# The opening of the first attention: one value group moved to the fifth pair, four masks with buffers of their own, and copies issued ahead of exponentials

## The reference, cut to what matters

```python
x = x + xattn0(layernorm(x), ctx, ctx, mask, Wq, Wk, Wv, Wo)   # 4 batches x 512 rows, 256 wide, 16 heads of 64
x = x + ffn0(layernorm(x), ...)                                # 8 experts, top-k by expert
x = x + xattn1(layernorm(x), ctx, ctx, ...)                    # banded, 16 heads of 16
x = x + ffn1(x, ...)                                           # 8 experts in 4 groups
# xattn0:
Qh, Kh, Vh = (q @ Wq, k @ Wk, v @ Wv)            # split into 16 heads
energy = einsum('nqhd,nkhd->nhqk', Qh, Kh) / 8
energy = where(mask == 0, -1e20, energy)
out = einsum('nhqk,nkhd->nqhd', softmax(energy), Vh).reshape(n, t, 1024) @ Wo
```

## Time and profile before

| | us |
|---|---|
| median of 3 runs | 1238.46 (1237.23 to 1240.76) |
| the profiled execution, its own time | 1239.35 |
| its span in the trace | 1237.6 |
| first attention | from 0 to about 510 |
| PE busy over the span | 1090.5 (88%) |
| mean granted clock of PE, of full speed | 0.938 |

### The profile page before, as it was taken

One profiled execution on the slowest core, in us unless ns is written; L12 is line 12 of the kernel. 1 busy time (PEld: TensorE's weight loads), 2 busy tenths in 40 slices (PEclk: granted clock), 3 DMA queues, 4 the chain that ended last, 5 costly groups with the idle time before them and its releaser, 6 DMA issues. The chain is left out here.

```text
span 1237.6 us, 28697 instructions
## 1 busy us (share of the span) xinstructions
PE 1090.5 (88%) x10304; PEld 807.7 (65%) x10305; DVE 743.5 (60%) x2145; ACT 684.8 (55%) x1300; POOL 516.9 (42%) x574
## 2 busy tenths in 40 slices
PE   5799999999999999975799996889898553999996
PEld 2567777777777777765488873445454242888885
DVE  5677876787778878756411045677776521555553
ACT  4788876787778777745422233576666211433331
POOL 4676455445554333210347620866665122121112
PEclk9899999999999999965899998999999765999998
DMA  9322222222212222164446556144442232111110
GB/s 312 88 69 54 53 70 69 53 53 70 66 48 60 55 53 53 27 206 139 125 147 192 152 136 207 52 122 121 137 127 75 95 95 69 27 30 26 21 27 10
DMA packets 89675, 111.01 MB, mean 90 GB/s; under 512 B 9744, under 2 KB 69904, under 8 KB 89424
## 3 DMA queue, kind: packets, MB, share of 16 engines
q1 hardware_dynamic: 82544, 100.88, 27.9%
q0 software_dynamic: 7008, 8.49, 3.9%
HBM read 59.93 MB, written 24.77 MB: 68 GB/s over the span
## 5 line engine op out<-in xcount | busy, mean ns | idle before, releaser
L638 DVE TENSOR_TENSOR e_t_lo<-et,e_t_hi 128x512 f16<-128x512 f32 x256 | 176.6, 690 | 55.4 <-ACT e_t_hi L558 52.9
L664 DVE CUSTOM_DVE_ANT_0 masked<-sc,mask_bias 128x512 f32<-128x512 f32 x256 | 175.6, 686 | 52.9 <-issue 39.1
L565 ACT ACTIVATE e<-masked,neg_max 128x512 f32<-128x512 f32 x256 | 184.3, 720 | 38.8 <-DVE neg_max L664 38.0
L558 ACT ACTIVATE e_t_hi<-et 128x512 f16<-128x512 f32 x256 | 151.9, 593 | 83.6 <-PE et L460 82.3
L460 PEld LDWEIGHTS et<-ident,e 128*128 128x128 f32 x1024 | 126.2, 141 | 53.6 <-ACT e L565 5.4
L460 PE MATMUL et<-ident,e 128*128 128x128 f32 x1024 | 154.5, 274 | 0.7 <-DVE e_t_lo L638 0.4
L1749 ACT ACTIVATE d_e<-d_st 128x384 f32<-128x384 f32 (+1 forms) x192 | 93.8, 526 | 50.4 <-PE d_st L1836 45.7
L84 PE MATMUL ob<-v_lo,e_t_hi 128*128 128x65 f16 x1024 | 119.5, 193 | 0.0
L83 PE MATMUL ob<-v_hi,e_t_hi 128*128 128x65 f16 x1024 | 119.3, 193 | 0.0
L85 PE MATMUL ob<-v_hi,e_t_lo 128*128 128x65 f16 x1024 | 118.7, 193 | 0.0
L2195 POOL DMA_INDIRECT out<-h_res,h_token x22 | 34.1, 1550 | 167.4 <-DVE h_res L2247 162.0
(11 more groups left out here) (393 smaller groups left out, 2800.5 us busy)
## 6 DMA issues: line engine op xcount, KB each, us to landing
kk<-nat_k SPq DMA_DIRECT2D x64, 256.0 KB, 3.5
raw<-in_fc SPq DMA_DIRECT2D x16, 1024.0 KB, 7.6
qq<-nat_q SPq DMA_DIRECT2D x64, 128.0 KB, 2.5
mask_raw<-in_mask SPq DMA_DIRECT2D x16, 256.0 KB, 3.5
scratch_stack<-kq_hi SPq DMA_DIRECT2D x16, 256.0 KB, 3.1
scratch_stack<-kq_lo SPq DMA_DIRECT2D x16, 256.0 KB, 3.2
q<-scratch_stack SPq DMA_DIRECT2D x32, 128.0 KB
k<-scratch_stack SPq DMA_DIRECT2D x32, 128.0 KB
```

The costliest lines, as they stand in the source:

```text
L558: nc.scalar.activation(e_t[u % NBUF].hi[:], et[u % 2][:], ACT.Copy).then_inc(turned_hi, 1)
L565: nc.scalar.activation(e[u % NBUF][:], masked[u % NBUF][:], ACT.Exp, bias=neg_max[:, g % 2, j:j + 1], scale=-1.0).then_inc(exp_ok, 1)
L638: nc.vector.tensor_tensor(e_t[u % NBUF].lo[:], et[u % 2][:], e_t[u % NBUF].hi[:], ALU.subtract).then_inc(turned_lo, 1)
L664: nc.vector.tensor_tensor_reduce(masked[u % NBUF][:], sc[j % 2][:], mask_bias[g // PAIRS % 2][:, j % QT, :], -SCALE0, 3e38, ALU.add, ALU.m ...
```

## The change

- **V groups.** V(1,0) moves from unit 4 of the first pair to unit 6 of the fifth pair. V(0,4) and V(0,6) move from units 0 and 1 to units 2 and 3.
- **Masks.** Masks 0 to 3 get four raw buffers (the two old ones and the two output tiles `o`) and semaphores of their own; masks 2 and 3 are loaded without waiting for POOL, right after `stack(0)`. Masks from 4 on use the two old buffers as before. POOL's place for mask 4 (unit 2) and SP's (behind `stack(1)`) are unchanged.
- **Parts.** `wv_b` is loaded after the masks instead of before `stack(0)`, and `ctx1` after `wk_b` and `wq_b`. High and low parts are made at units 3, 5, 6, 9, 13, 17, 21, 25, 29 and 33 (`SPLIT_AT0`). V(1,1), at unit 12, becomes the first group that needs `ctx1`. The constants of the second V tile move to the third pair.
- **ACT's order.** The high part of `wv_b` no longer stands before the first V group; in the first pair's units the copies out of `pj` stand ahead of the exponential.
- **DVE's order.** The low parts of Q0 and V(0,0) move ahead of one set of layer norm statistics each; that of V(0,2) moves behind the first maximum.

```diff
--- before.py
+++ after.py
@@ -93,14 +93,14 @@
         return "k", g + 1
     if j == 1 and g + 1 < PAIRS0:
         return "q", g + 1
-    if j == 4 and b + 1 < B:
+    if j == 4 and b + 1 < B and (b, p) != (0, 0):
         return "v", (b + 1, p)
     if j == 5 and b >= 1 and 1 <= p <= QT:
         return "w", (b - 1, p - 1)
     if j == 5 and b + 1 < B and p in NORM_PAIRS:
         return "z", (b + 1, p - NORM_PAIRS[0])
-    if j == 6 and b == 0 and p < QT:
-        return "v", (0, 2 * p + 1)
+    if j == 6 and b == 0 and p <= QT:
+        return "v", (0, 2 * p + 1) if p < QT else (1, 0)
     if j == 7 and g >= 1:
         return "t", g - 1
     return None
@@ -108,7 +108,7 @@
 
 def opening_work(u):
 
-    return ("v", (0, 2 * u + 4)) if u < 2 else None
+    return ("v", (0, 2 * u)) if 2 <= u <= 3 else None
 
 
 def is_direct(what):
@@ -131,11 +131,10 @@
 
 GROUP0, COPY0, ADD0, DIRECT0, ORDER0 = number_groups()
 EARLY = ("ctx0", "wk_a", "wq_a")
-PARTS0 = EARLY + ("wv_a", "wv_b", "ctx1", "wk_b", "wq_b", "wk_c", "wq_c", "ctx2", "ctx3", "wo_a", "wo_b")
+PARTS0 = EARLY + ("wv_a", "wv_b", "wk_b", "wq_b", "ctx1", "wk_c", "wq_c", "ctx2", "ctx3", "wo_a", "wo_b")
 PART0 = {name: n for n, name in enumerate(PARTS0)}
-SPLIT_LOW = {1: "wv_b", 2: "ctx1", 3: "wk_b", 5: "wq_b", 9: "wk_c", 12: "wq_c", 17: "ctx2", 20: "ctx3", 25: "wo_a", 28: "wo_b"}
-SPLIT_HIGH = {u: name for u, name in SPLIT_LOW.items() if name != "wv_b"}
-NEEDS = {("k", 2): "wk_b", ("q", 2): "wq_b", ("k", 4): "wk_c", ("q", 4): "wq_c", ("v", (1, 0)): "ctx1", ("v", (2, 0)): "ctx2", ("v", (3, 0)): "ctx3",
+SPLIT_AT0 = {3: "wv_b", 5: "wk_b", 6: "wq_b", 9: "ctx1", 13: "wk_c", 17: "wq_c", 21: "ctx2", 25: "ctx3", 29: "wo_a", 33: "wo_b"}
+NEEDS = {("k", 2): "wk_b", ("q", 2): "wq_b", ("k", 4): "wk_c", ("q", 4): "wq_c", ("v", (1, 1)): "ctx1", ("v", (2, 0)): "ctx2", ("v", (3, 0)): "ctx3",
          ("k", PAIRS): "ctx1", ("k", 2 * PAIRS): "ctx2", ("k", 3 * PAIRS): "ctx3", ("w", (0, 0)): "wo_b", ("v", (0, 1)): "wv_b"}
 
 
@@ -170,7 +169,8 @@
         scores, masked_ok, exp_ok = sem("scores"), sem("masked_ok"), sem("exp_ok")
         turned, turned_hi, turned_lo, pv_done = sem("turned"), sem("turned_hi"), sem("turned_lo"), sem("pv_done")
         rden_ok, normed = sem("rden_ok"), sem("normed")
-        mask_in, bias_ok = [sem(f"mask_in{i}") for i in range(2)], sem("bias_ok")
+        mask_in, bias_ok = [sem(f"mask_in{i}") for i in range(QT + 2)], sem("bias_ok")
+        early_masks = [mask_raw[0][:], mask_raw[1][:]] + [part[:].rearrange("p t d -> p (t d)").bitcast(I32) for part in o]
         last_turned, last_hi, last_lo, late_full = (sem(n) for n in ("last_turned", "last_hi", "last_lo", "late_full"))
         before_last = GROUP0["t", PAIRS0 - 2] % 2
         late = [sc[0], sc[1], pj[before_last], ob[0][:].rearrange("p t d -> p (t d)")]
@@ -243,9 +243,10 @@
             @block.sync
             def _(sp):
                 def load_mask(n):
-                    if n >= 2:
-                        sp.wait_ge(bias_ok, n - 1)
-                    sp.dma_start(mask_raw[n % 2][:], dram["mask"][n // QT, (n % QT) * P:(n % QT + 1) * P, :]).then_inc(mask_in[n % 2], 16)
+                    if n >= QT:
+                        sp.wait_ge(bias_ok, n - 3 if n < QT + 2 else n - 1)
+                    dst, done = (early_masks[n], mask_in[n]) if n < QT else (mask_raw[n % 2][:], mask_in[QT + n % 2])
+                    sp.dma_start(dst, dram["mask"][n // QT, (n % QT) * P:(n % QT + 1) * P, :]).then_inc(done, 16)
 
                 def stack(g):
                     i = g % 2
@@ -282,14 +283,10 @@
                 load_x(2)
                 load_mask(1)
                 load_x(3)
-                load_part("wv_b")
                 stack(0)
                 load_mask(2)
-                load_part("ctx1")
-                load_part("wk_b")
-                load_part("wq_b")
                 load_mask(3)
-                for name in ("wk_c", "wq_c", "ctx2", "ctx3", "wo_a", "wo_b"):
+                for name in ("wv_b", "wk_b", "wq_b", "ctx1", "wk_c", "wq_c", "ctx2", "ctx3", "wo_a", "wo_b"):
                     load_part(name)
                 for g in range(PAIRS0 - 1):
                     stack(g + 1)
@@ -299,10 +296,13 @@
             @block.gpsimd
             def _(pool):
                 def bias(n):
-                    pool.wait_ge(mask_in[n % 2], 16 * (n // 2 + 1))
+                    if n < QT:
+                        pool.wait_ge(mask_in[n], 16)
+                    else:
+                        pool.wait_ge(mask_in[QT + n % 2], 16 * ((n - QT) // 2 + 1))
                     if n >= 2 * QT:
                         pool.wait_ge(masked_ok, (n // QT - 1) * PAIRS * UNITS)
-                    pool.tensor_scalar(mask_bias[n // QT % 2][:, n % QT, :], mask_raw[n % 2][:], 0.0, MASKED, ALU.is_equal, ALU.mult).then_inc(bias_ok, 1)
+                    pool.tensor_scalar(mask_bias[n // QT % 2][:, n % QT, :], early_masks[n] if n < QT else mask_raw[n % 2][:], 0.0, MASKED, ALU.is_equal, ALU.mult).then_inc(bias_ok, 1)
 
                 def split(what):
                     kind, at = what
@@ -321,8 +321,8 @@
                         b, ct = at // PAIRS, at % PAIRS
                         if b >= 2:
                             pool.wait_ge(pj_full, GROUP0["w", (b - 2, QT - 1)] + 1)
-                        if b < 2:
-                            pool.wait_ge(part_lo, PART0["wq_b" if at == 0 else "wq_c" if at == 1 else "wo_b"] + 1 - len(EARLY))
+                        if b < 2 and at >= 1:
+                            pool.wait_ge(part_lo, PART0["wq_c" if b == 0 else "wo_b"] + 1 - len(EARLY))
                         hi, lo = o_t[b % 2].hi[:, ct, :], o_t[b % 2].lo[:, ct, :]
                     else:
                         pool.wait_ge(stacked[0], STACKED * at)
@@ -354,9 +354,9 @@
                         what = side_work(g, j)
                         if what in COPY0:
                             split(what)
-                        if g * UNITS + j in SPLIT_LOW:
-                            low_part(SPLIT_LOW[g * UNITS + j])
-                        if (g, j) == (0, 3):
+                        if g * UNITS + j in SPLIT_AT0:
+                            low_part(SPLIT_AT0[g * UNITS + j])
+                        if (g, j) == (2, 3):
                             pool.wait_ge(part_lo, PART0["ctx1"] + 1 - len(EARLY))
                             fill_constants(1)
                         if j == 2 and g // PAIRS + 1 < B and g % PAIRS < QT:
@@ -595,15 +595,14 @@
                 high_part("wv_a")
                 direct_high(("k", 0))
                 direct_high(("q", 0))
-                high_part("wv_b")
                 direct_high(("v", (0, 0)))
+                direct_high(("v", (0, 2)))
                 root(slice(QT, NT), 1)
-                direct_high(("v", (0, 2)))
                 units = PAIRS0 * UNITS
                 for u in range(units + TURN_LAG):
                     if u >= TURN_LAG:
                         turned_part(u - TURN_LAG)
-                    if u < units:
+                    if UNITS <= u < units:
                         exponent(u)
                     what = side_work((u - 1) // UNITS, (u - 1) % UNITS) if 1 <= u <= units else None
                     if what in COPY0:
@@ -612,8 +611,10 @@
                         direct_high(what)
                     if 1 <= u <= units and opening_work(u - 1) is not None:
                         direct_high(opening_work(u - 1))
-                    if u in SPLIT_HIGH:
-                        high_part(SPLIT_HIGH[u])
+                    if u < UNITS:
+                        exponent(u)
+                    if u in SPLIT_AT0:
+                        high_part(SPLIT_AT0[u])
                     ahead = side_work(u // UNITS, u % UNITS + 2) if u < units and u % UNITS == 3 else None
                     if ahead is not None and ahead[0] == "z":
                         b, i = ahead[1]
@@ -707,17 +708,17 @@
                     nc.vector.tensor_tensor(T.z_t.lo[:, :, cols], et[i][:].rearrange("p (c t) n -> p c (t n)", c=DT), T.z_t.hi[:, :, cols], ALU.subtract).then_inc(z_lo, 1)
                 statistics(1)
                 direct_low(("k", 0))
+                direct_low(("q", 0))
                 statistics(2)
-                direct_low(("q", 0))
+                direct_low(("v", (0, 0)))
                 statistics(3)
                 variances(later_tiles, 1)
-                direct_low(("v", (0, 0)))
-                direct_low(("v", (0, 2)))
                 units = PAIRS0 * UNITS
                 for u in range(units + TURN_LAG):
                     if u < units:
                         maximum(u)
                     if u == 0:
+                        direct_low(("v", (0, 2)))
                         scales(later_tiles, 1)
                     if u >= TURN_LAG:
                         turned_part(u - TURN_LAG)
```

## The result

| | before | after |
|---|---|---|
| median of 5 runs, us | 1238.46 (1237.23 to 1240.76) | 1246.11 (1244.38 to 1248.70) |
| the profiled execution's own time | 1239.35 | 1245.61 |
| span of that execution | 1237.6 | 1243.9 |
| ratio of the times | | 1.0064, 95% interval 1.0044 to 1.0084 |

The prediction, 1239.2 in a range of 1235.4 to 1243.0, was wrong: the sign was right, and so was the wait that it named, but the loss was 7.65 us and not 0.7.

What follows compares the result with a forecast made beforehand. It took PE as the bound, deciding when PE leaves its last long opening hole and with how much work ahead: 3.2 us later, minus 2.46 us, is +0.7, so 1238.46 + 0.7 = 1239.2 us, range 1235.4 to 1243.0.

Steps and rivals of the forecast that it cites:

- the sign: Whole kernel: slightly slower, 1238.46 + 0.7 = 1239.2 us.
- the wait that it named: First pair: POOL waits for mask 4's DMA, so PE idles before V(0,1) until 41.2 us, against 38.02 for V(1,0) before.
- The mechanism: Opening: mask 4 delays wv_b's low part and V(0,1) by 3.2 us; 2.46 us less work remains; half clock costs the same.
- the forecast of +0.7: Opening: PE resumes 3.2 us later with 2.46 us less work ahead, difference +0.7 us; chance 0.70.
- Mask 4's landing: DMA queue, first pair: mask 4 lands at 37.0 us, between 36.2 and 38.2, giving -0.1 to +1.9 us overall.
- V(1,1) and `ctx1`: Unit 12: POOL's step ends at 58.55, PE arrives at 59.17; 0.6 us of cover, up to 0.6 us if gone.
- The parts at units 13, 21 and 29: Parts made a few units later (13 to 33): same instructions, 2.13 us each on POOL, idle half the time; counted at nothing.
- The queue drains slowly: Slower rival: at 261 GB/s mask 4 lands at 41.7 us, PE starts at 45.9; +5.4 us, 1243.9; chance 0.12.
- The change does nothing to POOL's start: Rival: Q1 copy stays late, mask 4 issued at 35, landing at 37.8 us; +1.5 us, 1240; chance 0.08.
- Mask 4 doesn't queue: Faster rival: mask 4 lands at 31.8 us, PE starts at 36.1; -4.4 us, 1234.1; chance 0.10 together with no wait, 1231.
- The chance given to a loss: Whole kernel slower by over 0.3%: 0.12, and 0.02 for the forecast's upper tail; within 0.3%: 0.76.
- V(1,1) first: Condition for being wrong: PE waits again after 45 us, at V(1,1) before any other place.

Runs made afterwards that it cites:

- lows_first: Changed kernel with POOL taking mask 4 at unit 7 instead of unit 2 in the first pair; median 1241.22 us, ratio to the kernel before 1.0019.
- parts_late: Changed kernel with ctx2, ctx3, wo_a and wo_b loaded behind stack(1) and mask 4 instead of ahead; median 1242.87 us, ratio to before 1.0028.
- filled: Changed kernel with 48 products of 512 columns, result overwritten, added before the wait of V(0,1); median 1244.53 us, ratio to before 1.0048.
- v10_alone: Kernel before with only V(1,0) moved to unit 6 of the fifth pair; median 1234.10 us, ratio to before 0.9961.
- parts_at12: Changed kernel with mask 4 and ctx1 at unit 7, four parts behind mask 4, and wk_c, ctx2, wo_a at units 12, 20, 28; 1229.59 us, ratio 0.9930.
- all_three: Changed kernel with mask 4 and ctx1 at unit 7, and ctx2, ctx3, wo_a, wo_b loaded behind mask 4; median 1229.16 us, ratio to before 0.9911.
- ctx1_at7: Changed kernel with high and low part of ctx1 made at unit 7 instead of unit 9; median 1243.33 us, ratio to before 1.0038.

## Why the prediction was wrong

**The mechanism was right.** Mask 4's transfer became the last thing on POOL's way to `wv_b` (lows_first, parts_late), V(0,1) took the place of V(1,0) as the group that waits, half clock followed for as long as before in the profiled execution (filled has its price), and V(1,0) cost its 1.3 us later (v10_alone).

**Two terms were wrong, and a small one was missed.** Against the forecast of +0.7:

- *Mask 4's landing, +2.9.* The sum had 37.0, POOL began at 39.97 (38.58 to 40.40 in the four other executions with these loads, so +1.6 to +3.4). This is the step that failed first: "the DMA engines, not SP, set when this is through, at about 34.3" assumed that the new order moves the same bytes by the same time. By 34 us it had moved 0.6 MB less (295 against 313 GB/s), which is 1.7 us at 350 GB/s. I had capped the loss at 1.2 us, and then taken next to nothing of it. Why the bytes were fewer is shown only as far as the time: all of it was lost before 19 us, most of it from 14 to 16 us (86 against 359 GB/s), where the queue ran dry ahead of the first `kk`. The rest, about 1.2 us, is between the last bytes and the landing: 0.4 us as before was assumed, but the stages of the changed kernel show a tail:

```profile
37.00:38.00 1.00, 0.00 (x0) 0.00 (x0) 0.00 (x0) 0.00 (x0) 0.00 (x0) 0.50 0.99 269
38.00:39.00 1.00, 0.00 (x0) 0.00 (x0) 0.00 (x0) 0.00 (x0) 0.00 (x0) 0.50 0.26 86
39.00:40.00 1.00, 0.00 (x0) 0.00 (x0) 0.00 (x0) 0.00 (x0) 0.03 (x1) 0.50 0.03 10
```

  A transfer has landed when all 16 of its landing signals are in. The trace has those of mask 4 from 38.27 to 39.22, and the last alone at 39.89; before, all 16 came between 37.33 and 37.77. So the mean share is low there, 0.26 and 0.03, while the last engines still work.
- *V(1,1) and `ctx1`, +3.1.* This is a misread row. I took the V group at 59.17 for V(1,1) and found 0.6 us of cover. The group at 59.17 is V(0,3), of unit 14; V(1,1), of unit 12, is at 55.42 (two units of 1.23 and one group of 1.30 earlier, which is 3.75 us):

```profile
55.42 0.38 PE L83 MATMUL pj<-wv_hi,ctx_t_hi 128*128 128x512 f16 x1
```

  Against the end of POOL's step, 58.55, the cover is 55.42 - 58.55 = -3.1 us. The profile of before held this number to about a tenth (measured wait: 3.06). The mistake was not to count units from a known one to the row in hand.
- *The parts at units 13, 21 and 29, +0.7.* "The same instructions, hidden" was false for ACT: three waits of 0.45 grew to 0.70 to 0.72. parts_at12 shows the cause: one unit earlier, ACT's high part no longer follows the copy of a V group, and the waits are back at 0.45.

0.7 + 2.9 + 3.1 + 0.7 = 7.4, against a mark of 7.5 and 7.65 by the medians. That the sum agrees so well with both is in part luck: the ratio's interval is 2.5 us either way, and the first term alone differs by 1.8 us between executions.

Three smaller readings were off without effect, because mask 4's landing covered them: POOL ended masks 2 and 3 at 25.5 and not at 24, both splits at 29.1 and not at 27.8, and mask 4 was issued at 31.93 and not at 29.0.

**The rivals.** "The queue drains slowly" was the slower rival; its direction was right for mask 4 (39.9, not 41.7), but mask 4 alone would have left the time at about +3.6. "The change does nothing to POOL's start" fell: the splits ended 4.6 us earlier. "Mask 4 doesn't queue" fell with the 8.0 us from its issue to its landing and with parts_late. The sentence of the Trainium skill behind it (DMA: Bandwidth & Descriptors, Queues, rings and completion order) says two things: each engine takes its descriptors in ring order, and completion is not in order per issuing engine. With the first parts_late agrees, as far as one landing time can tell. Of the second no run here has a case in which mask 4 passed an earlier transfer.

**The chances.** The chance given to a loss was too low because three small terms had each been taken at the favourable end (0 to 1.2 taken near 0, a cover of 0.6, a cost of nothing), and all three went one way. "V(1,1) first", named as the place where I could be wrong, was the right place.

**What the change left unused.** With mask 4 and `ctx1` at other places in POOL's order and four late parts behind mask 4 on SP, the same change gives 0.9% (all_three). Its order frees POOL by 4.6 us and makes room on PE; v10_alone is one part of it and gives 0.4% by itself.

## What to carry to other kernels

When a step is moved ahead on an engine that works in order, look at the next wait behind it: here POOL was 4.6 us early, and then waited for a transfer that nobody needed for another 100 us, with the low parts of three weights behind it. Put steps that wait for the tail of a long DMA queue behind all that PE will ask for soon, and put early transfers ahead of bulk loads. To read from a timeline how much time a step has to spare (its cover), count from a step that is sure to the row in hand; repeated rows look alike.

## What the runs showed of the hardware

- A hole of 3 to 4 us on PE can cost more than its length: in lows_first, after holes of 4.08 and 3.05 us, the granted clock was at half (1.2 instead of 2.4 GHz) for over 3 us of full work, 1.7 us lost each. It need not: the hole of 3.06 us before V(1,1) in the changed kernel, as long, was followed by none; the granted clock reads 1.00 from 49 us on, and V(1,1)'s products take 0.38 us. With the 11.4 us hole filled by products without use, the next steps ran at 2.4 GHz and 1.9 us came back (filled).
- The same first products, ahead of all that the edit between these two kernels moves, went from 0.43 to 0.22 us apart at 11.7 us in one execution (ctx1_at7) and at 14.6 in another (after), while the column PEclk reads 1.00 throughout. With this the first `kk` was issued at 13.82 and at 14.66, and mask 4 taken at 38.58 and 39.97.
- 2.1 MB taken out from in front of a 256 KB transfer brought it 5.4 us forward: some 390 GB/s, close to the best stages (397), though in the stages of 1 us from 16 to 23 us, with `kk`, `qq` and the parts right after them, 160 to 321 GB/s move.
